# A two-layer transformer on one core: maxima turned ahead of the value burst, and a loop over head quads written out

## The reference, cut to what matters

```python
# first layer: the same logits are added to every head
logits = einsum('bnc,bmc->bnm', pre, pre) / sqrt(c)          # pre = silu(x @ Wpre + bpre)
score  = einsum('bhnd,bhmd->bhnm', q, k) / sqrt(dh)
attn   = softmax(pi[0] * logits[:, None] + score, axis=-1)
out    = einsum('bhnm,bhmd->bhnd', attn, v)
# second layer: 4 key/value groups, and a bias by relative position (constant beyond 127 steps)
scores = einsum('bhqd,bhkd->bhqk', q, k) + einsum('bhqd,kqd->bhqk', q, E[dist])
attn   = softmax(scores, axis=-1)
```

## Time and profile before

| | |
|---|---|
| median of 3 runs | 1612.63 us (1611.99 to 1632.21) |
| the profiled execution | 1619.09 us, of which the span is 1617.4 us |
| PE busy | 1357.1 us (84%) |
| PEld busy | 904.6 us (56%) |
| DVE busy | 893.8 us (55%) |
| ACT busy | 813.2 us (50%) |
| POOL busy | 661.8 us (41%) |
| first layer's attention, both batches | about 58 to 323 and 359 to 623 us of the span |
| second layer's attention | about 965 to 1550 us |

### The profile page before, as it was taken

The page is one execution under the profiler, slowest core; times in us unless marked ns, Lnnn a source line. Parts: engine busy times, 40 slices in busy tenths (PEclk is TensorE's granted clock), DMA queues, the critical chain, the costliest instruction groups (busy, mean ns, idle before and its releaser), DMA issues. The chain is left out here.

```text
span 1617.4 us, 39052 instructions
## 1 busy us (share of the span) xinstructions
PE 1357.1 (84%) x14415; PEld 904.6 (56%) x14415; DVE 893.8 (55%) x2426; ACT 813.2 (50%) x1571; POOL 661.8 (41%) x1281
## 2 busy tenths in 40 slices
PE   3999899989998997317999158999989999999967
PEld 1577677737776776215667124555545555555545
DVE  4566556446665665680233255666666666667652
ACT  2455455545554554100322255667666767777643
POOL 1466566516665662017154413334333334334400
PEclk9999999989999998558999666989998999999978
DMA  5610000052000000621253336666666566566600
GB/s 180 97 22 2 2 2 2 2 106 52 2 2 2 2 2 1 211 93 60 57 98 75 61 102 197 181 190 194 198 177 183 165 174 181 170 188 180 175 1 27
DMA packets 112815, 154.24 MB, mean 95 GB/s; under 512 B 15011, under 2 KB 98339, under 8 KB 111339
## 3 DMA queue, kind: packets, MB, share of 16 engines
q1 hardware_dynamic: 105851, 146.91, 33.0%
q0 software_dynamic: 6784, 4.87, 2.3%
HBM read 84.98 MB, written 66.46 MB: 94 GB/s over the span
## 5 line engine op out<-in xcount | busy, mean ns | idle before, releaser
L435 ACT ACTIVATE t_Pt<-t_psT 128x512 f32<-128x512 f32 x512 | 278.8, 596 | 242.4 <-PE t_psT L329 242.4
L377 DVE CUSTOM_DVE_ANT_0 t_Z<-t_psS,a0b_L 128x1024 f32<-128x1024 f32 x256 | 310.1, 1220 | 156.3 <-issue 150.7
L863 ACT ACTIVATE t_Pt<-t_psT 128x512 f32<-128x512 f32 x512 | 288.1, 596 | 160.8 <-PE t_psT L677 92.1
L765 DVE TENSOR_REDUCE t_mm<-t_psS 128x1 f32<-128x640 f32 (+1 forms) x256 | 219.6, 858 | 203.2 <-DMA t_A<-relative_rows 137.0
L329 PE MATMUL t_psT<-idf,t_Z 128*128 128x128 f32 x2048 | 283.6, 283 | 19.8 <-POOL t_Z L400 13.6
L400 POOL TENSOR_SCALAR t_Z<-t_Z,t_m 128x1024 f32<-128x1024 f32 x256 | 286.8, 1120 | 0.0
L329 PEld LDWEIGHTS t_psT<-idf,t_Z 128*128 128x128 f32 x2048 | 224.7, 144 | 107.4 <-issue 40.3
L663 PE MATMUL t_psS<-a1b_KT,a1b_QT 72*128 72x512 bf16 (+3 forms) x672 | 214.8, 348 | 5.6 <-DVE t_mm L766 5.4
L706 PE MATMUL t_psO<-t_Pt,t_Vh 128*32 128x128 f32 x4096 | 171.2, 287 | 3.6 <-DVE t_Os L789 3.6
L288 PE MATMUL t_psS<-a0b_KT,a0b_QT 72*128 72x512 bf16 (+1 forms) x512 | 155.3, 385 | 5.1 <-PEq L76 3.3
L834 POOL TENSOR_SCALAR t_neg<-t_m 128x4 f32<-128x4 f32 x64 | 14.1, 221 | 329.0 <-DVE t_m L775 329.0
(11 more groups left out here) (329 smaller groups left out, 1460.7 us busy)
## 6 DMA issues: line engine op xcount, KB each, us to landing
relative_rows<-t_rows SPq DMA_DIRECT2D x256, 192.0 KB, 2.9
t_A<-relative_rows SPq DMA_DIRECT2D x192, 192.0 KB, 3.2
t_A<-relative_rows SPq DMA_DIRECT2D x64, 128.0 KB, 2.4
a1b_QT<-query_parts SPq DMA_DIRECT2D x24, 192.0 KB
x_B<-in_b SPq DMA_DIRECT2D x1, 4096.0 KB, 18.1
x_A<-in_a SPq DMA_DIRECT2D x1, 4096.0 KB
a0b_QT<-query_parts SPq DMA_DIRECT2D x6, 576.0 KB
a0b_KT<-key_parts SPq DMA_DIRECT2D x18, 192.0 KB
```

The source lines that it names most:

```text
L377: nc.vector.tensor_tensor_reduce(out=Z[:, j, :], in0=psS[:, j % 2, :], in1=L[:, qt, :], scale=1.0, scalar=3e38, op0=ALU.add, op1=ALU.min, ...
L435: nc.scalar.activation(Pt[:, qt % 2, j, half * (N // 2):(half + 1) * (N // 2)], psT[:, half, :], ACT.Exp).then_inc(s_exp, 1)
L765: v.reduce_max(mm[:, u % AR, 1:2], psS[:, u % 2, width:N], AX)
L863: nc.scalar.activation(Pt[:, q % PR, :], psT[:, unit_item(G, i) % RR, :], ACT.Exp).then_inc(s_exp, 1)
```

## The change

The kernel is changed in four places. In `attend_quads` the loops on PE, DVE, POOL and ACT become Python loops, so that every quad is written out, and semaphore counts become constants. In `attend_direct` PE's extra item (`take`, `to_rows`, `turn_max`) moves ahead of the two pairs of `values`, which matters after i = 3, and DVE's `max_rows` (and `divide`) move from behind `tile(G + 2, 1)` to ahead of it. No arithmetic is added or removed.

```diff
--- before.py
+++ after.py
@@ -349,7 +349,7 @@
                 for i in range(3):
                     scores(0, i, i)
                 quad(0, first=True)
-                with pe.Fori(1, QUADS - 1) as hq:
+                for hq in range(1, QUADS - 1):
                     quad(hq)
                 quad(QUADS - 1, final=True)
                 values(QUADS - 1, QT_N - 1, False)
@@ -382,7 +382,7 @@
                             divide(hq - 1, 1)
 
                 quad(0, first=True)
-                with dve.Fori(1, QUADS) as hq:
+                for hq in range(1, QUADS):
                     quad(hq)
                 divide(QUADS - 1, 1)
 
@@ -406,7 +406,7 @@
                             nc.gpsimd.tensor_copy(Vh[:, :, :, 0:W], V[:, :, bass.ds(hq * J, J), :]).then_inc(s_vh, 1)
 
                 quad(0, first=True)
-                with pool.Fori(1, QUADS) as hq:
+                for hq in range(1, QUADS):
                     quad(hq)
 
             @block.scalar
@@ -435,7 +435,7 @@
                             nc.scalar.activation(Pt[:, qt % 2, j, half * (N // 2):(half + 1) * (N // 2)], psT[:, half, :], ACT.Exp).then_inc(s_exp, 1)
 
                 quad(0, first=True)
-                with act.Fori(1, QUADS) as hq:
+                for hq in range(1, QUADS):
                     quad(hq)
                 copy_out(QUADS - 1, 1)
 
@@ -730,21 +730,20 @@
                         else:
                             for part in ahead:
                                 scores(G + 2, i // 2, part)
-                        if i % 2:
-                            if G + 3 < GROUPS:
-                                relative(G + 3, i // 2)
-                            if i == 1 and G >= 1:
-                                values(G - 1, 6)
-                                values(G - 1, 7)
-                            if i > 1 and G >= 0:
-                                values(G, i - 3)
-                                values(G, i - 2)
+                        if i % 2 and G + 3 < GROUPS:
+                            relative(G + 3, i // 2)
                         if i == 3 and G >= -1:
                             out = take(extra_item(G), ("extra", G))
                             if G % 4 == 1 and G > 4:
                                 to_rows(G // 4 - 1, out)
                             if G + 1 < GROUPS:
                                 turn_max(G + 1, out)
+                        if i == 1 and G >= 1:
+                            values(G - 1, 6)
+                            values(G - 1, 7)
+                        if i > 1 and i % 2 and G >= 0:
+                            values(G, i - 3)
+                            values(G, i - 2)
                 values(GROUPS - 1, 6)
                 values(GROUPS - 1, 7)
                 to_rows(GROUPS // GRP - 1, take(extra_item(GROUPS), ("extra", GROUPS)))
@@ -801,17 +800,17 @@
 
                 for G in range(-2, GROUPS):
                     for j in range(J):
+                        if j == 1:
+                            if G >= -1 and G + 1 < GROUPS:
+                                max_rows(G + 1)
+                            if G % 4 == 1 and G > 4:
+                                divide(G // 4 - 1, extra_item(G))
                         if G + 2 < GROUPS:
                             tile(G + 2, j)
                             if j == J - 1:
                                 group_max(G + 2)
                         if j == 0 and G > 0 and G % GRP == 0:
                             copy_out(G // GRP - 1)
-                        if j == 1:
-                            if G >= -1 and G + 1 < GROUPS:
-                                max_rows(G + 1)
-                            if G % 4 == 1 and G > 4:
-                                divide(G // 4 - 1, extra_item(G))
                 copy_out(GROUPS // GRP - 1)
                 divide(GROUPS // GRP - 1, extra_item(GROUPS))
```

## The result

The changed kernel takes 1608.54 us, median of 20 runs (1597.33 to 1615.55). The kernel before, run beside it in as many, takes 1620.38 (1611.99 to 1635.72). The ratio is 0.9917 with a 95% interval of 0.9896 to 0.9937: 13.4 us less, about half of the 23.8 predicted. The profiled execution has 1608.73 us, against 1619.09 before.

What follows compares the result with a forecast made beforehand. PE was taken to bound the first layer and nearly the second, where SP's bias chain also holds it up. First layer -13.3, second -10.5, together -23.8 us from 1612.63, gave 1589.0 us; range 1576 to 1605 for 8 in 10.

Steps and rivals of the forecast that it cites:

- The base: Whole kernel: the gain was subtracted from the median of the runs, 1612.63 us, not from the profiled execution, 1619.09.
- The jumps: First layer: PE's backward jump per batch goes, 4.61 and 3.74 us, plus 2.45 each for half clock; 13.3 us.
- It is not seen to stall, so I take 0: First layer: written-out code on PE costs between 0 and 1.4 us in a quad, taken as 0.
- straight code is no faster: Rival, 0.05: PE pays the same 4.6 us somewhere in the first layer's written-out quads; 1602.1 us.
- (a): Second layer: PE's wait for the copy of the turned maxima goes, at most -18.8 us.
- (b): Second layer: PE newly waits for unit 2's exponential, 0.12 us in each of 63 groups, +7.6 us.
- (c): Second layer: the stall partly moves to PE's scores for DVE's tile, 0.7 us in three long waits, +2.1 us.
- (d): Second layer: half-clock stretches behind four of PE's waits go if the clock stays up, -11.9 us.
- The halving for SP: Second layer: SP's chain has no room in about half the cases, so half of 21.0 us is taken, -10.5.
- SP takes it all: Rival, 0.28: second layer's PE waits as long, at scores for `t_mm`; only the first layer gains; 1595 to 1603 us.
- The likeliest case: Chance 0.45: first layer gains as summed, second layer 4 to 16 us faster; 1583 to 1595 us.
- The slower rival: Rival, 0.05: second layer's DVE queues for PE's turned maxima, tile up to 0.87 us later per group; 1635.3 us.

Runs made afterwards that it cites:

- e17: Kernel before with the first layer's loops of DVE, POOL and ACT written out, PE's loop kept: one execution of 1621.62 us beside one of 1625.77.
- e16: Kernel before with the four loops written out and SP awaiting all key and query transfers before attention: one execution, 1691.8 us beside 1625.77.
- e7: Changed kernel with the three transfers of the turned maxima sent as one: ratio 0.9734 to the kernel before, 1575.49 us beside 1617.34.
- e6: Kernel before with the three transfers of the turned maxima sent as one: ratio 0.9802, 28.0 us off at the medians.
- e12: The changed kernel measured once more against the kernel before: ratio 0.9909, median 1614.95 us.
- e2: Kernel before with only PE's loop of the first layer written out: ratio 0.9957.
- e11: Kernel before with only the first layer's four loops written out, measured a second time: ratio 0.9950, median 1619.19 us.
- e3: Kernel before with only both moves of the second layer, loops kept: ratio 0.9967 (0.9926 to 1.0008).

## Why the prediction was off

**The base, 7.8 us of the 19.5 missed.** 1589.0 was subtracted from 1612.63, the median of three runs. The median of 20 is 1620.38. The profiled execution, 1619.09, had stood nearer to it all along; the step "I subtract from the median" chose the smaller sample. From the right base the sum would have been 1596.6, still 11.9 below the measured time.

**The jumps, right.** 4.61 and 3.74 us at the jumps and the half clock behind them are gone. Batch 1 gained 6.1 us where 6.2 was predicted, and was as short in every kernel with PE's loop written out. That the other three loops are worth nothing held too (e17). With 0.2 us for the jumps the first layer couldn't have gained the 6.1 of batch 1. The Trainium skill, "Advanced Engine Details and Errata", Control Flow Timing, has about 108 ns for a compare-and-branch; DVE's 50 to 69 ns lie below it and PE's 3795 and 4676 far above, as the rows had it.

**"It is not seen to stall, so I take 0" for straight code, wrong: 5.2 us back in batch 0.** The bound of 0 to 1.4 us was read from the last quad, which runs beside no transfers (DMA share 0.01). It said nothing of quad 0, where the transfers are, nor of blocks of instructions that can come late: PE stood 2.42 us there, until 3.24 us behind the start of such a block. So a part of the rival "straight code is no faster" came true: the stop is there, but in a quad that nobody rewrote, and in one batch of two. This and the jumps make 8.4 us in the timed runs instead of 13.3, 4.9 of the miss. The Trainium skill, "Runtime: NRT & Kernel Launch", Instruction fetch mechanics, has the cost of crossing a block in straight code mostly hidden; batch 1 and e16 agree, quad 0 of batch 0 doesn't.

**The second layer, right in direction and half in size: about 5 us instead of 10.5**, 5.5 of the miss. The 5 us are uncertain by nearly their own size, as said above. (The remaining 1.3 is that the medians of the two sets of runs differ by 11.8, where the ratio gives 13.4, less the rounding of the forecast.) By its terms, in this one pair of profiles:
- (a) -18.8: all of it went (one wait of 0.3 left at L655).
- (b) +7.6: measured 0.06 a group where PE is the bound, 3.7. In the changed kernel the waits for ACT at L713 and L719 are 4.3 us. The prediction has twice what was measured, since the 0.12 was read from one group. In e7 the stretch from the `relative` to unit 4 is 0.10 longer than in e6 at the median of the later groups without `to_rows`, in several of them not longer, and where `to_rows` stands 0.07 of it comes back before the next `relative`.
- (c) +2.1: mis-sized. 9.1 us came back at L663, in 15 waits and not in three. So what was wrong is that "only waits well beyond the average do this". That DVE's tiles came later than before, because a PE that runs ahead asks sooner for a bias that SP brings at its own pace, is the reading of it; no run here separates it.
- (d) -11.9: mis-sized. Summed from the clock records, the stage has 34.1 us at half clock instead of 37.5, so 1.7 us are saved. The drops follow other stops now, such as this one of 2.02 us in the kernel after:

```profile
1125.17 0.64 PE L706 MATMUL t_psO<-t_Pt,t_Vh 128*32 128x128 f32 x16
1127.83 0.38 PE L690 MATMUL t_psT<-a1b_QT,a1b_KT 75*128 75x512 bf16 x1 [2.02 <-DMA a1b_QT<-t_mr]
```

With the measured terms the sum is -18.8 + 4.3 + 9.1 - 1.7 = -7.1, where the profiles show 583.6 - 577.0 = 6.6; in e12, the same kernel, nothing of it is left. The halving for SP was then not an allowance on top of the terms; it is what (c) and (d) leave out. SP's chain was named as the reason, and e6 shows that it was the pace: a shorter chain takes 28 to 32 us off the kernel, and the reordering shows no more gain in the layer on top of it.

**The rival "SP takes it all", half right.** Its time, 1595 to 1603, would come to 1603 to 1611 on the right base, and the measured 1608.54 lies in it, in part by luck, since the first layer gave 8.4 us and not 13.3. Its mechanism is what the profile shows: PE waits at the scores for `t_mm` instead, and its waits together are 27.3 us where they were 31.5. The likeliest case, with a second layer 4 to 16 us faster, holds by the timed 5 us, at its lower edge.

**The slower rival, against.** DVE does stand in its queue for PE's turned maxima, 73.3 us in 57 waits of the stage, and its waits for the bias fall from the 119.3 us before to 83.5, but its waits for PE's scores fall too, from 61.0 to 24.9, and the three kinds together go from 186 to 182 us. So the copy's wait lies largely where the tile would have waited:

```profile
DVE t_mm L764 <- DMA t_A<-relative_rows: 83.5, 102, 2.5
DVE t_mr L781 <- PE t_psT L713: 73.3, 57, 3.0
```

## What to carry to other kernels

A wait that is moved ahead of the thing it waited behind can come back at the next place where the two engines meet, as half of it did here, unless what made it late is mended; here one line in the transfer queue was worth more than twice the whole change. Read the queue in order, find what fills it when it never waits for work, and shorten that first. When straight code is priced, read it in a stretch with the same transfers beside it. And take the base of a forecast from as many runs as there are: a median of three was off by 7.8 us, more than half of the effect.

## What was not expected of the hardware

- A backward jump of PE over one quad takes 3.8 to 4.7 us, of DVE 0.05 to 0.07, and the loss is real: writing out PE's loop alone gave 0.9957.
- PE stopped 1.1 to 4.7 us in straight code, from 82.8 to 84.8 us on, with no semaphore to wait for, in all thirteen profiles with its loop written out beside the large transfers. Each time it went on 3.15 to 3.64 us behind the start of an instruction transfer of 16384 bytes. It didn't stop with the large ones landed (e16), nor with the loop kept.
- One transfer of 12 rows of maxima holds SP's queue 0.74 us, three of 4 rows 1.84 (0.58 each at the median): the number of transfers costs far more than the rows in them.
- An unchanged second layer took 583.6 and 583.1 us in two profiles and 590.8 and 588.3 on other occasions (e2, e11), and the untouched part between the layers 343 to 355. With the new order it took 577.0, 575.2 (e3) and 591.7 (e12). Stage lengths of single profiles are no better than some 10 us between occasions; the ratios on one chip are what decides.
